# A 128-token-wide transformer block chain on one core: dummy matmuls of 512 columns placed in the waits of TensorE

## What is computed

```python
x = x + L0_xattn(_layernorm(x), ctx, ctx, mask)          # 16 heads of 8
x = x + L0_ffn(_layernorm(x))                            # self attention, then 4 mixed experts
x = x + L1_xattn(_layernorm(x), ctx, ctx, mask)          # 16 heads of 64
x = x + L1_ffn(_layernorm(x))                            # top 2 of 8 experts
x = x + L2_xattn(_layernorm(x), ctx)                     # 16 heads of 8
x = x + L2_ffn(_layernorm(x))                            # top 2 of 8 experts
x = x + L3_xattn(_layernorm(x), ctx)                     # two way attention
x = x + L3_ffn(_layernorm(x))                            # top 6 of 64 experts and a shared one
```

## Time and profile before

| | |
|---|---|
| median of 3 executions | 1598.68 us (1593.31 to 1598.70) |
| the profiled execution | 1598.73 us |
| its span, first to last instruction | 1596.8 us |
| PE busy | 1283.8 us (80% of the span) |
| DVE, ACT, POOL busy | 1024.7, 734.5, 620.8 us |
| mean granted clock of TensorE | 0.877 |

### The profile page before, as it was taken

The page is one execution under the profiler, slowest core; times in us unless marked ns, Lnnn a source line. Parts: engine busy times, 40 slices in busy tenths (PEclk is TensorE's granted clock), DMA queues, the critical chain, the costliest instruction groups (busy, mean ns, idle before and its releaser), DMA issues. The chain is left out here.

```text
span 1596.8 us, 24399 instructions
## 1 busy us (share of the span) xinstructions
PE 1283.8 (80%) x7148; PEld 1032.2 (65%) x7148; DVE 1024.7 (64%) x2047; ACT 734.5 (46%) x1260; POOL 620.8 (39%) x598
## 2 busy tenths in 40 slices
PE   4896669997997899721997499699946659999997
PEld 2673459987664599720886267588833438787875
DVE  3885678887324276660665466677768767667675
ACT  2443446665332554430654254455523325455553
POOL 1311634431000133245233131389844116676665
PEclk9996779999898899955999599699976669999998
DMA  3500011110000000131111100133202025343333
GB/s 89 143 0 1 0 41 36 39 39 5 1 0 0 20 1 0 60 112 55 35 48 32 44 1 0 45 97 97 95 19 103 1 60 125 109 130 115 126 115 104
DMA packets 69931, 85.64 MB, mean 54 GB/s; under 512 B 14282, under 2 KB 40269, under 8 KB 69850
## 3 DMA queue, kind: packets, MB, share of 16 engines
q1 hardware_dynamic: 67250, 79.94, 17.3%
q0 software_dynamic: 2272, 4.24, 0.8%
q10 hardware_dynamic: 336, 0.59, 0.2%
HBM read 69.98 MB, written 8.92 MB: 49 GB/s over the span
## 5 line engine op out<-in xcount | busy, mean ns | idle before, releaser
L2356 POOL TENSOR_TENSOR e_h<-e_h,e_gate 128x512 f32<-128x512 f32 x128 | 187.8, 1484 | 145.8 <-DVE e_h L2408 89.9
L2413 DVE TENSOR_TENSOR e_h_low<-e_h,e_h_high 128x512 fp32r<-128x512 f32 x132 | 117.8, 893 | 75.6 <-ACT e_h_high L2343 75.4
L2343 ACT ACTIVATE e_h_high<-e_h 128x512 fp32r<-128x512 f32 x132 | 83.5, 633 | 97.8 <-POOL e_h L2356 90.1
L228 PE MATMUL n_ps_t<-ident,n_zn 128*128 128x128 f32 x128 | 34.4, 433 | 90.5 <-DVE n_zn L167 82.7
L2408 DVE TENSOR_TENSOR e_h<-e_s,e_ps_b 128x512 f32<-128x512 f32 x132 | 89.4, 678 | 13.1 <-ACT e_s L2328 8.7
L1001 PE MATMUL u_ps_o<-u_vaug,u_pT 128*128 128x72 f32 x768 | 96.9, 269 | 0.0
L1001 PEld LDWEIGHTS u_ps_o<-u_vaug,u_pT 128*128 128x128 f32 x768 | 93.3, 192 | 0.0
L2328 ACT ACTIVATE e_s<-e_ps_a 128x512 f32<-128x512 f32 x132 | 77.7, 589 | 31.5 <-PE e_ps_a L1364 28.4
L228 PEld LDWEIGHTS n_ps_t<-ident,n_zn 128*128 128x128 f32 x128 | 23.9, 224 | 98.2 <-DVE n_zn L167 78.3
L932 POOL TENSOR_TENSOR u_kbd<-u_keys,groupmask 96x512 fp32r<-96x512 f32 x60 | 62.8, 1067 | 62.4 <-DMA u_keys<-s_k 37.2
L1028 ACT ACTIVATE u_sm<-u_sm 128x512 f32<-128x512 f32 x96 | 60.6, 631 | 54.5 <-DVE u_sm L1060 53.9
(11 more groups left out here) (439 smaller groups left out, 3901.3 us busy)
## 6 DMA issues: line engine op xcount, KB each, us to landing
e_gate<-gates_by_expert SPq DMA_DIRECT2D x256, 128.0 KB, 3.0
e_gate<-gates_by_expert SPq DMA_DIRECT2D x32, 256.0 KB, 3.4
w_raw<-in_L1w SPq DMA_DIRECT2D x24, 256.0 KB, 4.2
u_qs<-s_q SPq DMA_DIRECT2D x16, 192.0 KB, 2.6
u_keys<-s_k SPq DMA_DIRECT2D x8, 384.0 KB, 3.5
w_w<-in_L2w SPq DMA_DIRECT2D x24, 128.0 KB, 2.7
sorted<-blank SPq DMA_DIRECT2D x1, 2535.0 KB, 17.6
e_zb<-sorted SPq DMA_DIRECT2D x13, 195.0 KB, 2.5
```

The lines of the kernel that those rows point to most:

```text
L2343: nc.scalar.activation(h_parts[k % 3][0][:, :], h[k % 3][:, :], ACT.Copy).then_inc(high_ready, 1)
L2356: nc.gpsimd.tensor_tensor(h[c % 3][:, :], h[c % 3][:, :], gate[pair % SLOTS][:, :], ALU.mult)\
L2413: nc.vector.tensor_tensor(h_parts[k % 3][1][:, :], h[k % 3][:, :], h_parts[k % 3][0][:, :], ALU.subtract).then_inc(low_ready, 1)
```

## The change

A helper `keep_busy` issues a number of matmuls whose operands are both `ones_b` and whose output nobody reads: 512 columns each, the 128 ones read four times over. `normalise` gets one more PSUM bank, `spare`, and issues 36 of them on TensorE before it waits for the first group, and 4 ahead of each of the other three groups. `attend_two_way` issues 20 of them in each half, into the bank `ps_a[0]`, between the scores and the wait for `a_ready`. All nine normalisations get them.

```diff
+def keep_busy(nc, bank, ones, times):
+    for _ in range(times):
+        nc.tensor.matmul(bank[:, :].rearrange("p (a c) -> p a c", c=P), ones,
+                         ones.unsqueeze(1).broadcast_to([P, 4, P]), start=True, stop=True)
+
 def normalise(nc, tag, src, ident, root, out_T, center=True, second=None, out_natural=None, channel_scale=1.0,
...
-              meanwhile=None, before=None, rows=None):
+              meanwhile=None, before=None, rows=None, ones=None):
...
+        spare = m.ps("spare")
...
             if ident_loaded is not None:
                 pe.wait_ge(ident_loaded, 16)
+            keep_busy(nc, spare, ones, 36)
             for g in range(GROUPS):
+                if 0 < g:
+                    keep_busy(nc, spare, ones, 4)
                 pe.wait_ge(normed, g + 1)
...
-def attend_two_way(nc, tag, x, w, zT, ctxT, ctx_nat, ident, ones, many):
+def attend_two_way(nc, tag, x, w, zT, ctxT, ctx_nat, ident, ones, many, ones_b):
...
                     last.then_inc(s_done, 1)
+                keep_busy(nc, ps_a[0], ones_b, 20)
                 for r in seqs:
                     pe.wait_ge(a_ready, i * NS + r + 1)
```

More of the change, by code:

```diff
@@ L2563, in build @@
         normalise(nc, "n0_", x, idn, root_ln, zT, arrived=x_loaded, ident_loaded=ident_loaded, then=ACT.Exp,
-                  loads=load(first, first_loaded))
+                  loads=load(first, first_loaded), ones=ones_b[:, :])
         with ExitStack() as stack:
@@ L2608, in build @@
             normalise(nc, "n1_", x, idn, root_both, zT, second=root_ln, out_natural=x2,
-                      channel_scale=self_w["n1"][:, 0:1])
+                      channel_scale=self_w["n1"][:, 0:1], ones=ones_b[:, :])
             with ExitStack() as inner:
@@ L2617, in build @@
             normalise(nc, "n3_", x2, idn, root_rms, zT, center=False, channel_scale=self_w["n2"][:, 0:1],
-                      gate_w=self_w["gate"], logits=logits[4], then=ACT.Exp)
+                      gate_w=self_w["gate"], logits=logits[4], then=ACT.Exp, ones=ones_b[:, :])
             experts_mixed(nc, "e0_", x, x2, self_w, zT, logits[4], rank)
         clear_spent(nc)
-        normalise(nc, "n4_", x, idn, root_ln, zT, then=ACT.Exp)
+        normalise(nc, "n4_", x, idn, root_ln, zT, then=ACT.Exp, ones=ones_b[:, :])
         with ExitStack() as stack:
@@ L2634, in build @@
             normalise(nc, "n5_", x, idn, root_ln, zT, gate_w=gate1, logits=logits[8], then=ACT.Exp,
-                      loads=weights.first_loads, rows=rows[0])
+                      loads=weights.first_loads, rows=rows[0], ones=ones_b[:, :])
             experts_sorted(nc, "e1_", x, logits[8], rank, sort, weights, idn, rows, drams[0],
@@ L2638, in build @@
         clear_spent(nc)
-        normalise(nc, "n6_", x, idn, root_ln, zT, then=ACT.Exp)
+        normalise(nc, "n6_", x, idn, root_ln, zT, then=ACT.Exp, ones=ones_b[:, :])
         with ExitStack() as stack:
@@ L2651, in build @@
             normalise(nc, "n7_", x, idn, root_ln, zT, gate_w=gate2, logits=logits[8], then=ACT.Exp, parts=z,
-                      loads=weights.first_loads, meanwhile=weights.first_splits)
+                      loads=weights.first_loads, meanwhile=weights.first_splits, ones=ones_b[:, :])
             experts_gated(nc, "e2_", x, z, logits[8], rank, weights, idn, gates_dram, zT,
@@ L2656, in build @@
         many.make_room(m)
-        normalise(nc, "n8_", x, idn, root_ln, zT, then=ACT.Exp, before=lambda act: many.make_high(act, 0))
-        attend_two_way(nc, "t3_", x, two_way, zT, ctxT, ctx_nat, idn, ones[:, :], many)
+        normalise(nc, "n8_", x, idn, root_ln, zT, then=ACT.Exp, before=lambda act: many.make_high(act, 0), ones=ones_b[:, :])
+        attend_two_way(nc, "t3_", x, two_way, zT, ctxT, ctx_nat, idn, ones[:, :], many, ones_b[:, :])
         z = [m.sb(n, [P, TILES * P], F32R) for n in ("z_high", "z_low")]
         logits[64] = m.sb("logits64", [P, TILES, 64])
-        normalise(nc, "n9_", x, idn, root_ln, zT, gate_w=gate3, logits=logits[64], then=ACT.Sigmoid, parts=z)
+        normalise(nc, "n9_", x, idn, root_ln, zT, gate_w=gate3, logits=logits[64], then=ACT.Sigmoid, parts=z, ones=ones_b[:, :])
         experts_many(nc, "e3_", x, z, logits[64], bias3[:, :], many, idn,
```

## The result

| | before | after |
|---|---|---|
| median of the runs | 1596.41 us (4 runs, 1593.31 to 1598.70) | 1607.56 us (4 runs, 1604.99 to 1608.92) |
| profiled execution | 1598.73 us, span 1596.8 | 1604.99 us, span 1603.2 |
| mean granted clock | 0.877 | 0.915 |

The account below looks back on a forecast made before the run. Each normalisation was taken as one unhidden chain, TensorE waiting for VectorE's tiles and losing clock. 15.9 - 1.0 - 5.4 + 0.5 = 10.0 us more gave 1608.7 us, 0.63% slower; 8 in 10 range 1595 to 1617.

Parts of the forecast that it names:

- Part 1: 36 dummies ahead of the first group, no router: train takes 10.0 us, transposes 3.2 late; 15.9 more including later groups.
- Part 4: Stretches behind the normalisations: TensorE's clock, kept higher by the dummies, gives back 5.4 us, between 0 and 13.
- the rival of cheap dummies: Dummies at full clock cost less than 0.22 us, down to 0.12: 11 less, 1587.7 us; chance 0.08.
- Part 2: 4 dummies ahead of each later group, no router: faster transposes pay for them, 0.2 us more per block.
- Part 3: Four normalisations with a router: warm router matmuls and transposes cancel the late start, except n7, not late; 1.0 us less together.
- The late start of 1.0: Normalisations with a router: 36 dummies take 7.9 us against a wait of some 6.9, so transposes go 1.0 late each.
- the clock holds over the gaps: Full clock survives the 2.5 us gaps behind normalisations: 13 given back, not 5.4; 1601.1 us, no change; chance 0.22.
- Part 5: Two way attention: twenty dummies fit the transposes' waits, little gained; 0, plus 0.5 for half the first half's risk.

Follow-up runs that it names:

- the last two kernels: Changed kernel with 20 dummies without a router, 28 and 4 with one, self attention head filled, none two way; with 6 tail dummies 1581.60 us, without 1587.63 us.
- the plain ones alone: Kernel before with dummies only in the five normalisations without a router, none in the two way attention: 1613.29 us, ratio 1.0102.
- the kernel with ten behind: Trains cut to fit, none in the two way attention, plus 10 dummies behind the last transposes of normalisations without a router (3 in n1): 1581.86 us, ratio 0.9884.

## Why the prediction was right, and where its parts were not

1608.7 us were forecast and 1607.6 came, slower by 0.6% as forecast (11.2 us by the two medians). The total is right; its make-up is so in part, and one term of 8 us was not in it. That the total came out is luck: the terms that the forecast had come to 4.1 in place of 10.0, and a stretch that it did not look at made up the rest.

- **Part 1** held in kind: the train outlasts the wait, and the transposes queued behind it go late. It was oversized: 15.9 forecast, 12.7 measured (13.9 in the changed kernel's own profile). In its n4 the clock rose 3.0 us into the train (the windows under Part 4), not 4.35, so it took 9.39 us and not 10.0; in n1, n6 and n8 it rose after 4.1, 5.3 and 3.7. In three cases of the other profiles (n1 once, n8 twice) the train began at full clock and made the transposes only 1.2 late. Over the profiles a block was 2.1 to 3.0 longer, not 3.4. The dummies were 0.22 and 0.43 apart as the rows had it. The Trainium skill's sustained figure (page "TensorE: Matmul & The Clock Gate", section "Back-to-back issue gap", 0.131 us) was not seen, even in trains of 36, so the rival of cheap dummies is out. Cutting the train to 20 shows that Part 1 was the loss in these blocks.
- **Part 2** held: 4.54 in place of 4.51.
- **Part 3** was mis-sized: 1.0 less forecast, 4.5 measured. The late start of 1.0 was right for n5 (7.47 us in place of 6.50) and near for n9 (1.3); n3 was 2.2 late and gained nothing. What lies behind the start was 2.3 less in n5, not 1.0. And 36 was too long here as well: with 28 the four take 73.4 (mean of the last two kernels), 3.5 less again.
- **Part 4** held in size, not place by place: 5.4 forecast, 4.8 measured (0.5, 1.0, 1.7 and 1.6 behind n0, n3, n4 and n6). Behind n0 nothing was forecast; of the 1.5 behind n1 0.2 is seen in the one profile that could show it (246.5 with the plain ones alone). Its sum was off too: 1.2 twice, 1.5 and 1.0 are 4.9, not 5.4, and its bounds add up to 12.4, not 13, so by its own terms the forecast was 1609.2. That the clock holds over the gaps was a rival; in the changed kernel it held behind n6 (products from 915.0), and behind n4 it held over the gap and fell under the first products (from 537.25):

```profile
521.00:524.00 3.00, 2.97 (x8) 1.08 (x9) 2.72 (x17) 1.77 (x3) 0.00 (x0) 0.50 0.00 0
524.00:537.00 13.00, 10.76 (x58) 5.82 (x56) 6.67 (x31) 4.18 (x8) 0.00 (x0) 1.00 0.00 1
537.80:541.00 3.20, 3.20 (x5) 1.33 (x4) 0.00 (x0) 1.05 (x2) 0.00 (x0) 0.50 0.02 5
...
913.00:921.00 8.00, 6.03 (x26) 3.44 (x26) 1.23 (x1) 4.00 (x7) 0.00 (x0) 1.00 0.00 0
```

  So it goes either way from block to block, which the forecast's 1.2 each stood for. Nor do transposes leave the clock low each time, as the argument against this rival had it from n4: in n8 of the kernel before it was 0.50 from 1176.4 to 1180.9, with nothing on TensorE but the 16 transposes, and 1.00 from 1181.0.
- **Part 5** held: 0.5 forecast, no change that could be told.
- **What was missing:** 12.7 less 4.5, less 4.8, and 0.7 behind n8 are 4.1 more, in place of 10.0. The self attention adds 7.9: together 12.0, where the medians differ by 11.2. These are means over several kernels' profiles; the one pair of before and after has 13.9 less 4.5, 7.9 behind n1 and 10.9 less behind the other blocks, 6.4 in all, so the account is good to a few us. I looked for lost clock behind each block, and not at the attention that follows n1 70 us later. With its waits filled the change costs 0.7 us against before, and that includes a gain of 1.0 to 2.5 from the warm head (behind n1, 245.74 and 244.19 in place of 246.70), so without the long stretch the change costs 2 to 3 by this. The same two kernels with the head filled, without and with the change, are 5.1 apart by medians (1594.03 and 1599.12, on two chips).

Whether the change causes that stretch is only half settled. It stood in both profiles of kernels with all its dummies and the pause open, and by their times in four of six executions with the plain ones alone, and not in one that had executed the same instructions until then. So it differs from execution to execution, and by the times it is more frequent with the dummies than in the series of the kernel before. Why more frequent I can't show.

## What to carry to other kernels

Work that is issued ahead of a wait is not cut short when the wait ends, so it must be sized against the wait, and at the slow clock where the engine has stood idle: with 36 dummies the ratio was 1.0004, with 20 it was 0.9889 (both with the head of the self attention filled). A warm-up is worth what comes right behind it; the pauses to fill are those ahead of long solid stretches, and all of them, since one open pause of 2.9 us undid 20 dummies ahead of it (ratio 1.0100, and 1.0004 with it filled). Read the granted clock over the whole span, not around the edit alone, and take more than one profile before putting a few microseconds down to a stretch.

## What was not expected of the hardware

- TensorE at 100% busy is no guarantee of full clock: 22 us of fp32 products of 72 and 512 columns, fp32 transposes and short bf16 products, granted 0.50 throughout (94 matmuls where 181 fit). In the kernel before the clock rose within 3.4 us of the same work.
- The same instructions gave both outcomes: 254.6 us behind n1 in the changed kernel, 246.5 in the one with the plain dummies alone, which had executed the same until then.
- The clock can fall within a block that was just warmed: in the kernel with ten behind, n8's train ended at 1156, and the transposes of 1160.36 ran at half.
